# Order of TensorE's steps in the token stages of a two-layer block: probability transposes ahead of value products and row transposes

## The reference, cut to what matters

```python
q = _split_heads(query @ Wq.T + bq)
k = _split_heads(key @ Wk.T + bk)
v = _split_heads(value @ Wv.T + bv)
scores = jnp.einsum('bhqd,bhkd->bhqk', q, k)
scores = scores * tau[:, :, None, None] + delta[:, None, None, :]
scores = scores / jnp.sqrt(jnp.asarray(DK, scores.dtype))
p_attn = jax.nn.softmax(scores, axis=-1)
x = jnp.einsum('bhqk,bhkd->bhqd', p_attn, v)
x = x.transpose(0, 2, 1, 3).reshape(query.shape[0], -1, H * DK)
return x @ Wo.T + bo
```

## Time and profile before

| | |
|---|---|
| median of three runs | 3379.69 us |
| the profiled execution | 3375.24 us, its span 3373.5 us |
| TensorE, matmuls | 3187.6 us busy, 94% of the span |
| VectorE | 2720.3 us, 81% |
| GpSimd | 2097.0 us, 62% |
| ScalarE | 1560.8 us, 46% |
| granted TensorE clock, mean | 0.98 |

### The profile page before, as it was taken

How to read it: one execution, slowest core, us unless ns; L and a number is a source line. 1 busy time by engine, 2 the same in 40 slices (tenths; PEclk the granted TensorE clock), 3 DMA queues, 4 the chain that set the end, 5 groups by cost and what they waited for, 6 DMA issues and landing times. The chain is left out here.

```text
span 3373.5 us, 55546 instructions
## 1 busy us (share of the span) xinstructions
PE 3187.6 (94%) x17270; PEld 2498.1 (74%) x17270; DVE 2720.3 (81%) x5412; ACT 1560.8 (46%) x5463; POOL 2097.0 (62%) x2416
## 2 busy tenths in 40 slices
PE   7999999999979999999999699999999969999998
PEld 5677777777647888888888567777777758778886
DVE  4788888889746888888887389999999879967775
ACT  1766666676621111111111377777777745321111
POOL 1766766667635777777777477777777753433333
PEclk8999999999989999999999899999999989999999
DMA  7345454454465666766676444555554457730111
GB/s 219 100 137 169 119 172 134 141 155 134 136 210 131 167 176 165 179 168 166 166 179 155 111 128 135 159 164 144 150 171 136 138 166 287 274 102 13 26 13 25
DMA packets 285026, 491.01 MB, mean 146 GB/s; under 512 B 54258, under 2 KB 75058, under 8 KB 284018
## 3 DMA queue, kind: packets, MB, share of 16 engines
q1 hardware_dynamic: 252146, 409.92, 39.3%
q0 software_dynamic: 32256, 77.65, 12.3%
q10 hardware_dynamic: 384, 0.52, 0.1%
HBM read 250.32 MB, written 136.96 MB: 115 GB/s over the span
## 5 line engine op out<-in xcount | busy, mean ns | idle before, releaser
L984 ACT ACTIVATE c_pr<-ps,t_negmax 128x154 f32<-128x154 f32 x1024 | 384.8, 392 | 197.3 <-DVE t_negmax L731 196.3
L731 DVE TENSOR_REDUCE t_negmax<-ps 128x4 f32<-128x616 f32 x512 | 404.1, 789 | 53.2 <-PE ps L1053 52.7
L984 ACT ACTIVATE t_pr<-ps,t_negmax 128x154 f32<-128x154 f32 x1024 | 384.8, 392 | 107.9 <-DVE t_negmax L731 103.0
L754 DVE COPY t_pTm<-ps 128x512 f32<-128x512 f32 x448 | 306.2, 683 | 118.6 <-PE ps L1066 114.5
L649 POOL TENSOR_TENSOR t_pr<-t_pr,t_inv 128x512 f32<-128x512 f32 x256 | 274.8, 1073 | 191.0 <-DVE t_inv L746 189.9
L649 POOL TENSOR_TENSOR c_pr<-c_pr,t_inv 128x512 f32<-128x512 f32 x256 | 271.7, 1061 | 195.2 <-DVE t_inv L746 193.9
L1053 PE MATMUL ps<-t_kst,t_stack 98*128 98x154 f32 x2048 | 352.8, 291 | 26.7 <-DMA t_stack<-t_q_low 10.0
L1053 PEld LDWEIGHTS ps<-t_kst,t_stack 98*128 98x128 f32 x2048 | 279.5, 193 | 39.1 <-issue 18.3
L81 PE MATMUL ps<-e_xT_high,e_wgu_high 128*128 128x512 f32 x768 | 301.6, 393 | 1.4 <-DVE e_xT_low L1639 1.4
L83 PE MATMUL ps<-e_xT_high,e_wgu_low 128*128 128x512 f32 x768 | 299.3, 390 | 0.0
L82 PE MATMUL ps<-e_xT_low,e_wgu_high 128*128 128x512 f32 x768 | 299.0, 389 | 0.0
(11 more groups left out here) (359 smaller groups left out, 9313.8 us busy)
## 6 DMA issues: line engine op xcount, KB each, us to landing
t_stack<-t_q_high SPq DMA_DIRECT2D x1016, 64.0 KB, 2.0
c_wgu_in<-in_gate_upT SPq DMA_DIRECT2D x32, 1536.0 KB, 6.4
t_stack<-t_q_low SPq DMA_DIRECT2D x512, 64.0 KB, 2.0
x_dram<-c_wide_rows SPq DMA_DIRECT2D x32, 1024.0 KB, 7.6
c_wd_in<-in_downT SPq DMA_DIRECT2D x32, 768.0 KB, 11.5
t_xbo<-in_x SPq DMA_DIRECT2D x16, 1024.0 KB, 5.7
xw_dram<-t_z SPq DMA_DIRECT2D x16, 1024.0 KB, 5.3
t_xbo<-x_dram SPq DMA_DIRECT2D x16, 1024.0 KB, 11.2
```

What stands on the lines that cost most here:

```text
L731: dve.tensor_reduce(negmax[:, u, :], flat[:, at:at + HG * APART].rearrange("p (h n) -> p h n", h=HG)[:, :, 0:KEYS], AX, ALU.max, negate=Tr ...
L754: dve.tensor_copy(pTm[:, g % 2, :, t * P:(t + 1) * P], ps[:, 4, :].rearrange("p (h n) -> p h n", h=HG)).then_inc(s["pTm"], 1)
L984: op = act.activation(pr[:, u % 4, h, :], flat[:, col:col + KEYS], ACT.Exp, bias=negmax[:, u, h:h + 1], accum_out=total[:, u, h:h + 1])
```

## The change

In each odd slot of TensorE's order, `p_transposes` moves from the last place to the place behind the half product (`streamed`), in front of `values`, `x_turn`, `z_turn` and the gate's parts. Nothing else is touched.

```diff
@@ -1187,6 +1187,11 @@
                             scores(i, st, batch)
                     else:
                         streamed(st)
+                    if at % 2:
+                        if st < 2 and prev:
+                            p_transposes(i - 1, UNITS - 2 + st)
+                        if st >= 2 and cur:
+                            p_transposes(i, st - 2)
                     if at in V[:2] and cur:
                         values(i, V.index(at), batch)
                     if at in V[2:] and prev:
@@ -1199,11 +1204,6 @@
                         gate_parts(i - 2)
                     if at == GT and gate and prev2:
                         gate_turn(i - 2)
-                    if at % 2:
-                        if st < 2 and prev:
-                            p_transposes(i - 1, UNITS - 2 + st)
-                        if st >= 2 and cur:
-                            p_transposes(i, st - 2)
 
             unrolled(turn)
```

## The result

The changed kernel takes 3385.76 us (median of 20 runs, 3380.06 to 3393.11), the kernel before 3379.11 us (20 runs, 3375.39 to 3383.88). The ratio is 1.0020, 95% interval 1.0014 to 1.0027: some 4.7 to 9.1 us longer. The signs of three of the four terms were right; the fourth, a gain of 2.2 us, wasn't there, and two of the losses were put too high, so that the errors partly cancelled. Of all runs reported here, one of e9 (3929.28 us) and one of the kernel before (5225.82 us, taken beside e1 to e4) were far slower than the rest; the ratios leave them out.

The account below looks back on a forecast made before the run. TensorE's stream was taken to nearly fill both token stages, with a VectorE and GpSimd chain pacing the first up to step 5. Terms +0.6 + 3.4 - 2.2 + 2.4 = +4.2 us gave 3383.9 us; range 3375 to 3390.

Parts of the forecast that it names:

- the four terms: Seams +0.6 us, z's swap in the first stage +3.4, second stage's step 1 -2.2, end of second stage +2.4.
- the fourth: Second stage, step 1: earlier transposes let VectorE's maximum start sooner, -2.2 us over 13 groups.
- The seams: TensorE, reordered slots: 0.04 us more each, exposed only in step 7 of the first stage, +0.6 us.
- z in step 1: First stage: later z transposes delay rstd and x's normalizing, lengthening TensorE's step 5 wait; +0.24 a group, +3.4 us.
- Nothing gained: First stage, steps 3 and 7: transposes ahead of values end or can be copied sooner, but bring no gain.
- Second stage, step 1: Maximum starts some 0.17 us sooner, passed down VectorE's chain to step 13's wait; -2.2 us in 13 groups.
- End of the second stage: Last turn: transposes wait for GpSimd's tail and hold back the values; +2.4 us, bounds 0.8 and 2.4.
- The sum: Whole kernel: +0.6 + 3.4 - 2.2 + 2.4 = +4.2 us.
- Rival A: Slower, 3389.9 us: dearer seams, and z's full 0.46 us shift passes in step 1 of the first stage; chance 0.22.
- Rival B: Faster, 3367.9 us: feeding VectorE earlier shrinks or removes TensorE's step 5 wait in the first stage; chance 0.11.

Follow-up runs that it names:

- e9: Kernel before, first stage: x's last tile normalized in slot 11 instead of 7, z's third row copied in slot 13 instead of 11; 3433.05 us, ratio 1.0150.
- e1: Changed kernel, but the first-stage slots with z's row transposes keep the old order; 3383.39 us, ratio 1.0015.
- e4: Changed kernel, but values stay ahead of transposes in step 7 of the second stage's first group; 3386.67 us, ratio 1.0023.
- e5: Kernel before, with probability transposes ahead of z's transposes in step 1 of the first stage alone; 3382.61 us (one run).
- e6: Kernel before, with probability transposes ahead of z's transposes in step 2 of the first stage alone; 3379.06 us (one run).
- e10: Kernel before, with transposes ahead of values in step 3 of the first stage alone; 3378.74 us, ratio 0.9996.
- e2: Kernel before, with probability transposes ahead of z's transposes in steps 1 and 2 of the first stage alone; 3381.66 us, ratio 1.0009.
- e7: Kernel before, with three of six products of the half product left out in step 2 of the second stage's groups; 3379.63 us (one run).
- e8: Changed kernel, with three of six products of the half product left out in step 2 of the second stage's groups; 3385.16 us (one run).
- e3: Changed kernel, but transposes stay behind values in the turn after the second stage's last group; 3384.7 us, ratio 1.0019.
- e11: The changed kernel once more, with no further edit; 3388.05 us (11 runs), ratio 1.0021.
- e12: Kernel before, with transposes ahead of values in step 3 of the first stage and experts marked in slot 15 instead of 9; 3362.0 us, ratio 0.9941.

## Why the forecast was right in its number, and where its steps were not

**The seams** (0.04 each): right. By the table, steps 7 and 8 of the first stage take 7.24 us instead of 7.19, steps 1 and 2 of the second 6.81 instead of 6.76. Values and z's transposes start 0.11 us behind the start of L1066, scores 0.02 (2223.66 to 2223.68 in the earlier trace rows). The rule of the Trainium skill that was weighed there ("TensorE: Matmul & The Clock Gate", The mechanism), that a weight load overlaps running matmuls only where the row group differs, doesn't fit this trace: in the earlier trace rows loads are busy 36.52 us and matmuls 48.94 of the same 50, so they overlap for over 35 us by the modelled ends, though the weights of the products all stand in the same 128 rows; in step 1 the products start 0.23 us apart and each has a load of 0.19 beside it. The conclusion drawn from it, that no order would cost anything more, isn't borne out either: 0.05 was measured. Why a seam costs what it does stays open.

**z in step 1** (+0.24 a group): right in mechanism and sign. The wait for z was 0.32 us (0.28 forecast), the late rstd held the normalizing as described, by 0.39. The term was oversized since the normalizing itself got 0.17 shorter when it started later, and since the copy behind it had been held for 0.11 by the transposes, not by the normalizing; and it missed that the swap in step 2 leads to the same join. e5 and e6 show both; together +0.15 a group.

**"Nothing gained"** in step 3 of the first stage: wrong. The step that failed is "VectorE is in its 2.86 us and copies at 616.44 anyway". The 0.03 us between the end of the normalizing and the copy, which I had noted and dismissed, was the sign that the copy was held by something else: by the transposes, whose end was 616.40. Unheld, VectorE starts a copy some 0.07 us before the recorded end of the work in front (e10). Worth 0.14 us a group by itself; in the changed kernel the late normalizing swallows nearly all of it: the copy comes 0.13 us late there and 0.15 in e2, which has z's swaps alone (medians over the groups). TensorE's wait fell to 7.9 us, where 13 was forecast, mostly for another reason. TensorE comes to it 0.17 us later itself, by 0.10 in step 2 and the seams of steps 3 and 4 (676.07 - 0.60 - 54.28 = 621.19, against 621.69 - 0.67 = 621.02), and so more than the 0.10 by which the wait ends later. A shorter wait was no gain here. The kernel before, and the changed one:

```profile
621.69 0.63 PE L1065 MATMUL ps<-ident,c_pr 128*128 128x128 f32 x4 [0.67 <-DVE t_pTm L754]
```

```profile
676.07 0.63 PE L1065 MATMUL ps<-ident,c_pr 128*128 128x128 f32 x4 [0.60 <-DVE t_pTm L754]
```

**Second stage, step 1** (-0.17 a group): wrong, at "It passes down the chain" and, in front of it, at the reading that VectorE works without a wait from there to step 12. The maximum of step 2 did come 0.18 us early, as worked out. But two later joins had TensorE as their other input, ready within 0.1 us of VectorE's own stream, and the rows showed no wait for either: the maximum of step 3 (its scores) and the copy behind the transposes of step 4. At the second TensorE's stream sets the pace, before the change (by the 0.1 us that an unheld copy would start sooner) as after it, and there the gain ended. The group grew by 0.03, the seams'. e7 and e8 bear this out: with TensorE's stream sooner from step 3 on, the difference of the two orders is -0.14 us a group, close to the -0.17 forecast.

**End of the second stage** (+2.4): right in place, and 2.45 us in the profiled pair. That it fits so well is in part luck: the kernel before had been profiled with one of the shortest half-clock stretches there, and the changed one with a long one. It is +1.6 on average over all profiles, and 0.75 to 1.2 where the clock is alike (see e3).

**The sum.** By the first normalize of a group, over several profiles of each order: third to sixteenth group of the first stage, 697.3 us (changed kernel, e3, e4, e8, e11) instead of 694.6 (before and e7), +2.6; second to sixteenth of the second stage, 707.7 (changed kernel, e1, e3, e4, e11) instead of 706.7 (seven kernels with the old order), +1.1; last turn +1.6. Together +5.3 us, inside the measured 4.7 to 9.1. What is missing to the medians' 6.65 isn't attributed. It may be more than 1.3: e1 measured +3.8 us, and its parts give -1.5 (14 x -0.11) + 1.1 + 1.6 = +1.2. Its lower bound of 1.7 is above that. In e4 and e8 the half clock lasts until 14 us behind the last normalize, and the part behind the last values takes 652.0 and 654.6 us, where it takes 644.0 to 649.3 in all other profiles; both have the new order in the last turn. That may be a part of what is missing, but two of five profiles don't show that the order brings it about. Stretches without any edit differ by more than that from profile to profile, so single profiles can't settle it, and it stays open. The forecast of 4.2 came as near as it did by luck in part, since losses that were too large (3.4 and 2.4) and a gain that wasn't there (-2.2) partly cancelled. Rival A's sign was right; its cause, dearer seams and the full shift of z, was not. Rival B's idea, that feeding VectorE sooner frees TensorE, holds in one slot, step 3, and there for another reason.

**The bound now.** The Trainium skill ("Perfetto Trace Analysis", Optimization Strategy) says to find the gaps on the engine that is to be filled and what ends them, and then to make those dependencies start sooner or complete faster. By e10 and e12 this is right here only if followed through each join: the gap of step 5 was ended by VectorE's copy, and its chain had the transposes, the normalizing, the scores of step 4 and the marking within some 0.2 us of one another.

## What to carry to other kernels

A wait of zero in a trace isn't slack. Before a gain is passed down a chain, look at every later join for its other input and its time; a difference of under 0.1 us between both is a tie, and both sides have to move. Go on past the first such join: in the second stage the gain was still there behind the first and ended at the second. And a wait that shrinks need not be a gain, since the engine may only have come to it later. Moving an early delivery in front of long work pays where the receiver is held by just that delivery, and costs where it delays another; so decide slot by slot, and look for what holds the chain next, since the larger gain may lie there (here 0.14 us a group from the order, 0.94 more with the marking moved).

## What the runs showed of the hardware

- VectorE's copy of transposes (L754), when nothing holds it, starts 0.07 to 0.09 us before the recorded end of the instruction in front (e10, 669.32 against 666.54 + 2.85; in the kernel before 247 copies between 100 and 2700 us do). A copy that starts just after that end is a sign of something that held it. Other pairs have other spacings: the first L717 behind a L710 starts 0.05 us after the end each time, so the comparison is with the same pair elsewhere in the trace.
- VectorE's time for the same instruction depends on what GpSimd does beside it. The cast at L70 took 0.39 us where GpSimd did nothing (kernel before, 603.65), 1.51 in e10, beside a bias addition (L696), and 0.91 in e12, beside a normalize (L649). The Trainium skill ("GPSIMD Engine Reference", Specifications) says that GpSimd shares its SBUF interfaces with VectorE, with contention where VectorE's instruction is in a two-port mode or has two SBUF inputs. The three durations agree with the sharing; this cast has one input, and which mode it runs in no run here shows. Part of e12's gain in step 5 is this:

```profile
672.18 1.34 POOL L696 TENSOR_TENSOR t_xbo<-t_xbo,t_bo 128x512 f32<-128x512 f32 x1
```

```profile
672.30 1.51 DVE L70 CAST t_q_high<-t_qT 128x512 fp32r<-128x512 f32 x1
```

- The half clock in a thin stretch is not the same from run to run: the same kernel took 46.49 and 44.59 us for one group (after and e11), with the granted clock at 0.50 for 10 us of it in one and for under 4 in the other.
- A wait of 2.3 us on TensorE in the steady groups cost 4.7 us a group (e9), since the granted clock was 0.50 behind it; the waits of 0.6 to 0.7 us in step 5 had no such stretch behind them.
